# A fused transformer layer on one core: banks for the norm transposes, tables for additions and norms, order of the late norms

## The chip, the cores and the metric

The kernel runs on one core of a Trainium2 chip. The metric is the device time of one execution in microseconds (us), the median of several executions. The engines are TensorE (PE, and PEld for its weight loads), VectorE (DVE), ScalarE (ACT), GpSimd (POOL) and SyncE (SP, which issues most transfers). Each runs its own instructions in order; between engines the order is made by semaphores only.

## What is computed

The input x is 16 x 64 x 512 in float32, that is 1024 tokens of 512 features, handled as 8 tiles of 128 tokens.

```
x = x + cross_attention(layernorm(x), ctx, mask)      # 16 heads, 1601 context rows per batch
x = x + self_attention(layernorm(x))                  # w_qkv + b_qkv, low-rank terms on q and v, w_proj + b_proj
x = x + moe(layernorm(x))                             # gate: gelu(x @ wg1 + bg1) @ wg2 + bg2, softmax, top 2 of 20
```

The self attention works on each batch of 64 tokens alone, so a tile of 128 tokens holds two batches. The mixture of experts multiplies each token with the 512 x 512 matrices of its two best experts.

## The kernel before

Every float32 product is made of three products of rounded halves (`mm3`, lines 178 to 181), so each operand is kept as a high half (ScalarE copies it, L728) and a low half (VectorE subtracts, L1051). A product of one tile with a 512 x 512 weight is 12 matmuls (L179 to L181) into one PSUM bank of 512 columns. PSUM has 8 banks, `pb[0]` to `pb[7]`.

**Cross attention** fills the first 480 us and is not touched. **Before the steps** (lines 1344 to 1374 on VectorE) the layernorm of the second attention is made: residual addition and statistics per tile, factors on GpSimd (`factors`, L1617 and L1618), the norm on ScalarE (L878), a transpose on TensorE (L185), the halves, and the products that make queries and keys. `weight2(2, 1)` is VectorE's low half of the key weight, 128x2048; it stands ahead of `norm_lo(4)` and `norm_lo(5)`, and `keys2` waits for it.

**The second attention** is a loop over 14 steps, with three stages of eight tiles laid over one another:

- step s: scores of tile s (`a_scores`, L540, banks 4 to 7), the softmax on VectorE (L1380, L1386), ScalarE's exponential (L965), sums on VectorE and scaling on GpSimd (L1640);
- step s for tile s-1: the weights are turned (`a_turn`, L550) into banks 2 and 3, and ScalarE copies each bank (semaphore `a_t2`);
- step s for tile s-2: the product with the values (`a_values`, L566, in columns of banks 4 to 7), whose result ScalarE copies (L983) and VectorE halves (L1423, semaphore `v_h2`).

**Beside** them stand dense uses of TensorE, in a table `beside` (lines 679 to 685), three lists a step: values `v2`, output products `pj` (L582), norm transposes `n2` (L586) and the gate products `g1` (lines 591 to 597). They take banks 0 and 1 in turn, in the order of the table (line 691). A use waits until the use before it in the same bank has been read: `before` looks that up. Who reads what is in `done`: a `pj` is read by VectorE's residual addition (L1405, semaphore `v_x2`), a `v2` by ScalarE's copy, an `n2` by VectorE's low half (`v_n2`), a `g1` by `gelu`.

The addition for `pj` i stands one step later than the product, behind that step's softmax on VectorE, and ahead of the `n2` halves of the step; after it come the statistics, the factors on GpSimd, the norm on ScalarE one step later than the product (`norms(step - 1)`), behind the copies L983, and its transpose `n2` at the end of that step.

The order of the last steps before: `pj` 5, 6 and 7 stand in steps 9, 10 and 11, `n2` 4 and 5 in steps 9 and 10, the first gate product in step 11, `n2` 6 and 7 in step 12, the second gate product in step 13. On ScalarE `gelu(0)` comes in step 11 ahead of the norm of tile 7, the high half of expert weight 1 (`we_hi(1)`) at the end of step 12, then `gelu(1)`. On VectorE the low half `we_lo(1)` (L1436) stands behind the loop and ahead of the wait for the logits (L1448). `gelu` is a line of its own (L937) with a table load. SyncE loads the expert weights in a queue; those of 1 to 8 start when `p_a2` reaches 8, the last `a_values`.

**After the steps** come the logits (L617), a chain of small VectorE instructions (L1448 to L1505), GpSimd's 16 scatters of tokens (L1656), 20 or more expert blocks, and the gathers and last additions.

Of the kernel before, what the change touches and what calls it, by code (L numbers as in the profile page):

```python
# [17 lines left out]
def perceiver(nc, t, out):  # L18
# [9 lines left out]
    with root:  # L28
# [223 lines left out]
        def tensor(pe):  # L252
# [291 lines left out]
            def a_turn(i):  # L544
                for h in range(2):
                    pe.wait_ge(S["g_p2"], 2 * i + h + 1)
                    if i:
                        pe.wait_ge(S["a_t2"], 2 * i - 1 + h)
                    for j in range(4):
                        last = pe.transpose(pb[2 + h][:, j * 128:(j + 1) * 128],  # L550
                                            p2[i % 2][:, 4 * h + j].rearrange("p b k -> p (b k)"), ident)
                    last.then_inc(S["p_t2"], 1)
# [18 lines left out]
            def dense(what, i):  # L571
                if what == "qd":
                    queries2(1, i - 4)
                elif what == "kT":
                    keys2(1, i - 4)
                elif what == "v2":
                    values2(i)
                elif what == "pj":
                    pe.wait_ge(S["v_w2"], 2)
                    pe.wait_ge(S["v_h2"], i + 1)  # L580
                    pe.wait_ge(*before("pj", i))
                    project(i, wh[0], pb[bank_of("pj", i)]).then_inc(S["p_pj"], 1)  # L582
                elif what == "n2":
                    pe.wait_ge(S["a_nx"], 8 + i + 1)
                    pe.wait_ge(*before("n2", i))
                    turn4(pe, pb[bank_of("n2", i)], lambda k: xrow[:, i, k * 128:(k + 1) * 128]).then_inc(S["p_n2"], 1)  # L586
                else:
                    pe.wait_ge(S["v_g1"], 1)
                    pe.wait_ge(S["v_n2"], 8 + 4 * i + 3)
                    pe.wait_ge(*before("g1", i))  # L590
                    for c in (slice(0, 384), slice(384, 512)):
                        if c.start:
                            pe.wait_ge(S["v_n2"], 8 + 4 * i + 4)
                        for k in range(4):
                            last = mm3(pe, pb[bank_of("g1", i)][:, c], [w[:, k, :] for w in g1],
                                       [v[:, k, i * 512 + c.start:i * 512 + c.stop] for v in xu], k == 0, k == 3)
                    last.then_inc(S["p_g1"], 1)
# [76 lines left out]
            while guards:  # L674
# [11 lines left out]
        step_of = {use: step for step, parts in enumerate(beside) for part in parts for use in part}  # L686
        STEPS = len(beside)
        ring = [("o", i) for i in range(EARLY, 8)] + [("qd", m) for m in range(4)]
        ring += [use for m in range(4) for use in (("wl", 4 + m), ("kT", m))] + [("qd", 4)]
        place = [(("wl", k), 4 + k) for k in range(4)] + [(use, n % 3) for n, use in enumerate(ring)]  # L690
        place += [(use, n % 2) for n, use in enumerate([use for step in beside for part in step for use in part])]
        bank = dict(place)
        done = {"wl": ("v_wl", 0), "o": ("v_x1", 0), "kT": ("a_kT", 0), "v2": ("a_v2", 0),
                "pj": ("v_x2", 0), "n2": ("v_n2", 8), "g1": ("a_gelu", 0)}
# [31 lines left out]
        def scalar(act):  # L726
# [214 lines left out]
            def beside_read(uses):  # L941
                for what, i in uses:
                    if what == "qd":
                        queries2(1, i - 4)
                    elif what == "kT":
                        keys2(1, i - 4)
                    elif what == "v2":
                        values2(i)
                    elif what == "n2":
                        act.wait_ge(S["p_n2"], i + 1)  # L950
                        copy(xu[0][:, :, i * 128:(i + 1) * 128], kview(pb[bank_of("n2", i)])).then_inc(S["a_n2"], 1)
                    elif what == "g1":
                        gelu(i)

            def norms(step):
                for i in range(8):
                    if step_of["pj", i] == step:
                        norm(8 + i, i, xrow[:, i, 0:D])

            for step in range(STEPS):  # L960
                if step < 8:
                    i = step
                    pv = p2[i % 2].rearrange("p t b k -> p (t b k)")
                    act.wait_ge(S["v_sm"], 2 * i + 2)
                    act.activation(pv, pv, ACT.Exp, scale=SCALE).then_inc(S["a_e2"], 1)  # L965
                beside_read(beside[step][0])
                if 0 <= step - 1 < 8:
                    i = step - 1
                    for h in range(2):
                        act.wait_ge(S["p_t2"], 2 * i + h + 1)  # L970
                        if i >= 2:
                            act.wait_ge(S["p_a2"], i - 1)
                        else:
                            act.wait_ge(S["p_wl"], 8)
                        copy(pt2[:, i % 2, 4 * h:4 * h + 4, :].rearrange("p a c -> p (a c)"),
                             pb[2 + h][:, :]).then_inc(S["a_t2"], 1)
                beside_read(beside[step][1])
                if 0 <= step - 2 < 8:
                    i = step - 2
                    c = slice(i * 128, i * 128 + 128)  # L980
                    act.wait_ge(S["p_a2"], i + 1)
                    for g in range(4):
                        ins = act.activation(xu[0][:, g, c].rearrange("p (b q) -> p b q", b=2), turned2[:, :, g // 2, g % 2],  # L983
                                             ACT.Identity, bias=bl[:, 4 + g:5 + g])
                        if g % 2:
                            ins.then_inc(S["a_h2"], 1)
                norms(step - 1)
                beside_read(beside[step][2])
                if step == 3:
                    act.wait_ge(S["d_g1"], 32)  # L990
                    copy(g1[0][:, :, :], g1raw).then_inc(S["a_g1"], 1)
                if step == 5:
                    we_hi(0)
                if step == 12:
                    we_hi(1)

            act.wait_ge(S["v_lg"], 1)
            act.activation(pr[:, :, :], pr[:, :, :], ACT.Exp).then_inc(S["a_le"], 1)
# [48 lines left out]
        def vector(dve):  # L1047
# [286 lines left out]
            def weight2(j, n):  # L1334
                dve.wait_ge(S["a_w2"], n)
                rest(wh[j][1][:, :, :], raw[:, 0], wh[j][0][:, :, :]).then_inc(S["v_w2"], 1)
# [24 lines left out]
            norm_lo(2)  # L1361
            norm_lo(3)
            out_add(7)
            weight2(2, 1)
            norm_lo(4)
            norm_lo(5)
            queries2(0, 1)
            norm_lo(6)
            norm_lo(7)
# [27 lines left out]
            for step in range(STEPS):  # L1397
# [1 line left out]
                    i = step  # L1399
                    a_softmax(i)  # L1400
                for i in range(8):
                    if step_of["pj", i] == step - 1:
                        dve.wait_ge(S["g_xb"], i + 1)
                        dve.wait_ge(S["p_pj"], i + 1)
                        dve.tensor_tensor(x_sb[:, i, :], x_sb[:, i, :], pb[bank_of("pj", i)][:, :],  # L1405
                                          ALU.add).then_inc(S["v_x2"], 1)
                        dve.wait_ge(S["v_x2"], i + 1)
                        stat(i)
# [151 lines left out]
        def gpsimd(pool):  # L1560
# [70 lines left out]
                pool.wait_ge(S["g_xb"], i + 1)  # L1631
            for i in range(STEPS):
                for j in range(8):
                    if step_of["pj", j] == i - 1:
                        factors(8 + j, j)
                if i < 8:
                    pool.wait_ge(S["v_rl2"], i + 1)
                    for h in range(2):
                        pv = p2[i % 2][:, 4 * h:4 * h + 4].rearrange("p t b k -> p (t b) k")
                        pool.tensor_tensor(pv, pv, ls2[:, i % 3, 8 * h:8 * h + 8].unsqueeze(2).to_broadcast([128, 8, 64]),  # L1640
                                           ALU.mult).then_inc(S["g_p2"], 1)
                if i in (6, 7):
                    pool.wait_ge(S["a_we"], 1)
                    pool.wait_ge(d_we[0], 16)
                    for k in (2 * (i - 6), 2 * (i - 6) + 1):
                        ins = pool.tensor_tensor(wsplit[0][1][:, k, :], wraws[0][:, k, :],
                                                 wsplit[0][0][:, k, :].bitcast(f32), ALU.subtract)
                    if i == 7:
                        ins.then_inc(S["g_we"], 1)
# [312 lines left out]
```

## Time and profile before

| what | us |
|---|---|
| median of 3 runs | 831.63 (831.05 to 832.65) |
| the profiled execution's own time | 832.59 |
| its span, first to last instruction | 830.8 |
| PE busy | 723.9 (87%) |
| DVE busy | 402.4 (48%) |
| ACT busy | 365.1 (44%) |
| POOL busy | 279.7 (34%) |

All durations come from the one profiled execution. "Busy" is the time in which an engine works; the chain that ended last has PE in 75% of the span. A line of the timeline gives start, duration, engine, line of the kernel, operation, out<-in with shapes, count, and in brackets the idle time before it with what ended it. Matmuls overlap in the profile, so a start to the next start is the pace.

### The profile page before, as it was taken

Reading aid. Unit: us, or ns where it says so; the run is one execution under the profiler, and the core shown is the slowest. Engines: PE = TensorE matmul, PEld = TensorE weight load, DVE = VectorE, ACT = ScalarE, POOL = GpSimd, SP = SyncE. Lnnn points to the kernel's source line nnn. Section 1 sums busy time; section 2 is a strip of 40 time slices with the busy share of each in tenths; the row PEclk is TensorE's granted clock in tenths of the full one; section 3 lists DMA queues with packets and bytes.
Section 4 is the critical chain, followed back from the end, with each engine's and each line's share of the span. In section 5 each row is a group of like instructions: output and inputs, shape, how many; then the busy total and the mean of one; then the engine's idle time right before and its main releaser. Section 6 shows DMA issues by size and latency. Waiting matters only on the chain.

```text
span 830.8 us, 16898 instructions
## 1 busy us (share of the span) xinstructions
PE 723.9 (87%) x6819; PEld 586.9 (71%) x6819; DVE 402.4 (48%) x846; ACT 365.1 (44%) x665; POOL 279.7 (34%) x249
## 2 busy tenths in 40 slices
PE   0899999999999999999999999999686653989880
PEld 0797888878888888888788777877564621766660
DVE  4823443354444345444543283446533452677755
ACT  1425534545434454445453163444442400688750
POOL 0005223444224442245542236022321044243334
PEclk9999999999999999999999999999998755899995
DMA  9303321453322333101100021100007426499938
GB/s 292 120 1 44 86 54 38 131 136 85 86 82 56 85 85 85 41 2 40 42 2 2 4 66 64 52 2 2 2 1 285 191 101 203 153 374 415 390 126 305
DMA packets 43783, 89.98 MB, mean 108 GB/s; under 512 B 7370, under 2 KB 26314, under 8 KB 39214
## 3 DMA queue, kind: packets, MB, share of 16 engines
q1 hardware_dynamic: 40254, 77.46, 29.5%
q0 software_dynamic: 3440, 11.31, 3.4%
q8 instruction: 58, 0.95, 0.5%
q14 instruction: 31, 0.25, 0.1%
HBM read 66.18 MB, written 22.65 MB: 107 GB/s over the span
## 4 chain that ended last, share of the span: by engine, by line
PE 75%; DMA 8%; DVE 6%; issue 6%; ACT 3%; POOL 2%; SPq 0%; POOLq 0%; DVEq 0%; ACTq 0%
PE bank L179 20%; PE bank L181 18%; PE bank L180 18%; PE bank L185 9%; PE bank L338 4%; PE bank L315 3%; DMA xi<-scratch_xg 3%; POOL scratch_xg L1656 2%; DMA scratch_ys<-xm,xi 2%; DVE x_sb L1555 1%; DMA scratch_ys<-hT,xi 1%; DMA scratch_xg<-acc,si 1%; PE bank L550 1%; DMA wr<-scratch_ys 1%; ACT xu L728 1%
## 5 line engine op out<-in xcount | busy, mean ns | idle before, releaser
L1583 POOL TENSOR_SCALAR pp<-pp,rl 128x400 f32<-128x400 f32 x128 | 163.8, 1298 | 234.8 <-DVE rl L1148 234.8
L179 PE MATMUL bank<-chi,wk 128*128 128x400 f32 x256 | 93.5, 365 | 0.0
L1204 DVE COPY pt<-bank 128x512 f32<-128x512 f32 x64 | 44.3, 692 | 99.4 <-PE bank L185 99.3
L811 ACT ACTIVATE pp<-pp,acc 128x400 f32<-128x400 f32 x128 | 79.0, 619 | 28.0 <-DVE acc L1237 27.7
L1237 DVE CUSTOM_DVE_ANT_0 pp<-bank,cap 128x400 f32<-128x400 f32 x128 | 66.8, 569 | 46.5 <-PE bank L315 46.5
L181 PE MATMUL bank<-chi,wk 128*128 128x400 f32 x256 | 88.3, 345 | 0.0
L180 PE MATMUL bank<-clo,wk 128*128 128x400 f32 x256 | 88.3, 345 | 0.0
L179 PE MATMUL bank<-wv,chi 128*128 128x512 f32 x200 | 83.5, 417 | 0.0
L179 PE MATMUL bank<-wh,xu 128*128 128x512 f32 x152 | 66.9, 440 | 16.8 <-DVE x_sb L1405 15.8
L181 PE MATMUL bank<-wv,clo 128*128 128x512 f32 x200 | 78.5, 393 | 0.0
L180 PE MATMUL bank<-wv,chi 128*128 128x512 f32 x200 | 78.5, 393 | 0.0
L728 ACT ACTIVATE pt<-bank 128x512 f32<-128x512 f32 x64 | 38.2, 597 | 76.4 <-PE bank L185 75.3
L185 PE MATMUL bank<-cst,pp 128*128 128x128 f32 x512 | 67.2, 274 | 0.6 <-DVE x_sb L1181 0.6
L181 PE MATMUL bank<-wh,xu 128*128 128x512 f32 x152 | 63.6, 418 | 0.0
L180 PE MATMUL bank<-wh,xu 128*128 128x512 f32 x152 | 63.5, 418 | 0.0
L185 PEld LDWEIGHTS bank<-cst,pp 128*128 128x128 f32 x512 | 58.5, 140 | 5.8 <-issue 0.8
L728 ACT ACTIVATE vv<-bank 128x512 f32<-128x512 f32 x50 | 29.1, 583 | 64.9 <-PE bank L181 64.9
L179 PEld LDWEIGHTS bank<-wv,chi 128*128 128x128 f32 x200 | 37.5, 188 | 27.9 <-issue 19.4
L1051 DVE TENSOR_TENSOR xu<-bank,xu 128x512 fp32r<-128x512 f32 x44 | 29.9, 687 | 44.7 <-ACT xu L728 44.7
L1135 DVE COPY kk<-bank 128x400 f32<-128x400 f32 x32 | 18.4, 575 | 63.3 <-PE bank L181 63.3
L179 PEld LDWEIGHTS bank<-wh,xu 128*128 128x128 f32 x152 | 30.8, 203 | 24.7 <-issue 18.4
L180 PEld LDWEIGHTS bank<-clo,wk 128*128 128x128 f32 x256 | 48.3, 189 | 0.0
(224 smaller groups left out, 1424.4 us busy)
## 6 DMA issues: line engine op xcount, KB each, us to landing
wr<-in_We SPq DMA_DIRECT2D x19, 1024.0 KB, 8.9
craw<-in_ctx SPq DMA_DIRECT2D x16, 800.0 KB, 5.7
scratch_xg<-zero SPq DMA_DIRECT2D x20, 448.0 KB, 8.3
raw<-in_We SPq DMA_DIRECT2D x8, 1024.0 KB, 7.6
xi<-scratch_xg SPq DMA_DIRECT2D x28, 258.0 KB, 6.6
wr<-scratch_ys SPq DMA_DIRECT2D x8, 512.0 KB, 7.3
x_sb<-in_x SPq DMA_DIRECT2D x2, 1024.0 KB, 12.1
out_dram<-x_sb SPq DMA_DIRECT2D x8, 256.0 KB, 4.2
```

The costliest lines, as they stand in the source:

```text
L179: pe.matmul(o, lhs[0], rhs[0], start=start, stop=False)
L180: pe.matmul(o, lhs[0], rhs[1], start=False, stop=False)
L181: return pe.matmul(o, lhs[1], rhs[0], start=False, stop=stop)
L185: last = pe.transpose(bank[0:n, k * 128:(k + 1) * 128], of(k), ident)
L315: last = pe.matmul(scores[64 * c:64 * c + 64, j, :], qc[r, 2 * half + c, 64 * b:64 * b + 64], kk[r, 2 * half + c, :], start=True, stop=True)
L338: last = pe.matmul(turned[32 * j:32 * j + 32, g, :], vv[:, (25 * (n // 8) + 3 * (n % 8) + i4) % 4, 128 * g + 32 * j:128 * g + 32 * j + 32] ...
L728: return act.activation(dst, src, ACT.Copy)
L811: act.activation(frame(p8), frame(p8), ACT.Exp, bias=bias, scale=-1.0, accum_out=total).then_inc(S["a_exp"], 1)
L1051: return dve.tensor_tensor(dst, src, hi.bitcast(f32), ALU.subtract)
L1204: dve.tensor_copy(pt[:, p8 % 4, :, :].rearrange("p a c -> p (a c)"), at("t", 8 * (n - 1) + p8)[:, :]).then_inc(S["v_pt"], 1)
L1237: dve.tensor_tensor_reduce(out=frame(p8), in0=scores[:, p8 % 4, :], in1=cap[:, :], scale=-1.0, scalar=nm[:, b, p8:p8 + 1] if seg else 3e38 ...
L1583: pool.tensor_scalar(frame(p8), frame(p8), rl[:, n % 2, p8:p8 + 1], None, ALU.mult).then_inc(S["g_pn"], 1)
```

## The change

On TensorE the transposes `n2` no longer take banks 0 and 1 but banks 2 and 3, those of the turned weights. Each waits for ScalarE's last copy of a turned half in its bank and for the `n2` two before it; each `a_turn` in turn waits for the last `n2` of its bank. Banks 0 and 1 go round among the other uses. Tables say in which step an addition and a norm stand; the addition for `pj` 7 moves from step 12 to step 11. `n2` 6 moves into step 11, `n2` 7 is alone in step 12. On ScalarE the norms of the steps from 8 on come ahead of the copies L983, `gelu(0)` moves to the end of step 12, and `we_hi(1)` comes behind `gelu(1)`. On VectorE `weight2(2, 1)` comes behind `norm_lo(4)` and `norm_lo(5)`. GpSimd's factors follow the table of additions. `we_lo(1)` keeps its place on VectorE.

```diff
--- before.py
+++ after.py
@@ tensor: a_turn
                     if i:
                         pe.wait_ge(S["a_t2"], 2 * i - 1 + h)
+                    turned = [j for j in range(8) if j % 2 == h and step_of["n2", j] <= i]
+                    if turned:
+                        pe.wait_ge(S["v_n2"], 8 + turned[-1] + 1)
@@ tensor: dense
                 elif what == "n2":
                     pe.wait_ge(S["a_nx"], 8 + i + 1)
-                    pe.wait_ge(*before("n2", i))
+                    pe.wait_ge(S["a_t2"], 2 * min(step_of["n2", i] - 1, 7) + i % 2 + 1)
+                    if i >= 2:
+                        pe.wait_ge(S["v_n2"], 8 + i - 1)
@@ tables
-                  ([("pj", 6)], [], [("n2", 5)]), ([("pj", 7)], [], [("g1", 0)]),
-                  ([], [], [("n2", 6), ("n2", 7)]), ([], [], [("g1", 1)])]
+                  ([("pj", 6)], [], [("n2", 5)]), ([("pj", 7)], [], [("g1", 0), ("n2", 6)]),
+                  ([], [], [("n2", 7)]), ([], [], [("g1", 1)])]
+        add_at = {i: step_of["pj", i] + (i < 7) for i in range(8)}
+        norm_at = {i: step_of["pj", i] + 1 for i in range(8)}
...
-        place += [(use, n % 2) for n, use in enumerate([use for step in beside for part in step for use in part])]
+        dense_uses = [use for step in beside for part in step for use in part if use[0] != "n2"]
+        place += [(use, n % 2) for n, use in enumerate(dense_uses)]
+        place += [(("n2", i), 2 + i % 2) for i in range(8)]
@@ scalar
-                    elif what == "g1":
-                        gelu(i)
...
-                    if step_of["pj", i] == step:
+                    if norm_at[i] == step:
...
                 beside_read(beside[step][1])
+                if step >= 8:
+                    norms(step)
                 if 0 <= step - 2 < 8:
...
-                norms(step - 1)
+                if step < 8:
+                    norms(step)
                 beside_read(beside[step][2])
...
                 if step == 12:
-                    we_hi(1)
+                    gelu(0)
+            gelu(1)
+            we_hi(1)
@@ vector, ahead of the steps
             out_add(7)
-            weight2(2, 1)
             norm_lo(4)
             norm_lo(5)
+            weight2(2, 1)
             queries2(0, 1)
@@ vector, in the steps
-                    if step_of["pj", i] == step - 1:
+                    if add_at[i] == step:
@@ gpsimd
-                    if step_of["pj", j] == i - 1:
+                    if add_at[j] == i:
```

## Rows read from the trace of the kernel before

**Rows 1.** Stretches: each engine's busy us, PE clock share, DMA share, GB/s.

```profile
583.60:597.80 14.20, 10.49 (x169) 8.44 (x168) 7.30 (x15) 6.87 (x11) 5.26 (x6) 0.88 0.01 2
630.00:637.40 7.40, 5.26 (x18) 4.04 (x19) 2.38 (x6) 1.41 (x2) 0.74 (x2) 0.77 1.00 404
660.90:673.70 12.80, 2.23 (x8) 1.67 (x8) 10.56 (x60) 2.14 (x2) 0.00 (x0) 0.50 0.01 2
```

**Rows 2.** Waits of PE, 574 to 664 us: total, times, longest.

```profile
PE bank L179 <- DVE x_sb L1405: 15.8, 6, 3.7
PE bank L185 <- ACT acc L878: 4.3, 2, 2.3
```

**Rows 3.** Timeline, steps 6 to 8: start, us, instruction, [idle before].

```profile
587.51 1.06 ACT L965 ACTIVATE acc<-acc 128x1024 f32<-128x1024 f32 x1 [1.41 <-DVE acc L1386]
...
588.22 0.47 PE L179 MATMUL bank<-wh,xu 128*128 128x512 f32 x1 [3.71 <-DVE x_sb L1405]
...
592.63 0.60 PE L550 MATMUL bank<-cst,p2b 128*128 128x128 f32 x4
...
614.12 0.47 PE L179 MATMUL bank<-wh,xu 128*128 128x512 f32 x1 [2.10 <-DVE x_sb L1405]
...
617.00 1.03 PE L550 MATMUL bank<-cst,p2b 128*128 128x128 f32 x8
```

**Rows 4.** Timeline, one norm's way in step 10.

```profile
637.23 0.60 PE L185 MATMUL bank<-cst,acc 128*128 128x128 f32 x4
637.86 0.60 ACT L728 ACTIVATE xu<-bank 128x512 fp32r<-128x512 f32 x1 [2.27 <-PE bank L185]
638.49 0.69 DVE L1051 TENSOR_TENSOR xu<-bank,xu 128x512 fp32r<-128x512 f32 x1 [4.65 <-ACT xu L728]
639.10 0.68 DVE L1405 TENSOR_TENSOR x_sb<-x_sb,bank 128x512 f32<-128x512 f32 x1
...
641.05 0.55 POOL L1617 TENSOR_TENSOR rstd<-rstd,cst 128x1 f32<-128x1 f32 x1 [6.31 <-DVE nbias L1311]
...
641.90 0.81 ACT L878 ACTIVATE acc<-x_sb,nbias,rstd 128x512 f32<-128x512 f32 x1 [3.45 <-POOL nbias L1618]
```

**Rows 5.** Timeline around the two gate products, steps 11 to 13.

```profile
644.34 0.34 PE L179 MATMUL bank<-xu,g 128*128 128x384 f32 x1
...
647.75 0.62 PE L185 MATMUL bank<-cst,acc 128*128 128x128 f32 x4
647.98 1.28 ACT L937 ACT_TABLE_LOAD   x1 [5.26 <-PE bank L181]
...
650.71 1.12 PE L185 MATMUL bank<-cst,acc 128*128 128x128 f32 x4 [2.34 <-ACT acc L878]
...
652.02 0.66 PE L179 MATMUL bank<-xu,g 128*128 128x384 f32 x1 [0.19 <-DVE xu L1051]
```

**Rows 6.** Timeline ahead of the steps, last norms of the first attention.

```profile
494.99 0.55 POOL L1617 TENSOR_TENSOR rstd<-rstd,cst 128x1 f32<-128x1 f32 x1 [3.79 <-DVE nbias L1311]
...
498.69 2.28 DVE L1051 TENSOR_TENSOR wh<-raw,wh 128x2048 fp32r<-128x2048 f32 x1
...
498.86 2.53 POOL L1617 TENSOR_TENSOR rstd<-rstd,cst 128x1 f32<-128x1 f32 x1 [3.04 <-DVE nbias L1311]
...
504.43 0.63 PE L185 MATMUL bank<-cst,acc 128*128 128x128 f32 x4 [1.24 <-DVE xu L1051]
```

**Rows 7.** Timeline, from the gate to the first scatter.

```profile
652.36 1.90 ACT L728 ACTIVATE wh<-raw 128x2048 fp32r<-128x2048 f32 x1
...
654.30 2.29 DVE L1436 TENSOR_TENSOR wh<-raw,wh 128x2048 fp32r<-128x2048 f32 x1 [1.11 <-ACT wh L728]
...
658.12 0.69 ACT L937 ACTIVATE xm<-bank,gw 128x512 f32<-128x512 f32 x1 [3.86 <-issue]
...
660.91 0.33 DVE L1448 TENSOR_TENSOR pr<-bank,bro 128x160 f32<-128x160 f32 x1 [4.32 <-PE bank L617]
...
674.04 1.27 POOL L1656 DMA_INDIRECT scratch_xg<-acc,si  x1 [26.64 <-DVE si L1505]
```

## The prediction

> **What bounds the kernel now.** I began with the page of the profile: PE is busy in 87% of the span and holds 75% of the chain that ended last, so a wait of PE on this chain is time to be won. The page's slices then show where PE isn't full: in the second attention's late steps, and behind them in the routing. The windows by stage put numbers on it: from 583.6 to 597.8 us PE works 10.49 of 14.2 us at a granted clock of 0.88, from 630.0 to 637.4 it works 5.26 of 7.4 us at 0.77 [rows 1]. The list of waits names the causes: six matmuls waited 15.8 us in all for VectorE's residual addition L1405, and norm transposes waited 4.3 us for ScalarE's norm L878, twice [rows 2]. The timeline shows what such a wait is. In step 6 the product `v2` 5 sits in the bank that held `pj` 1, whose addition stands behind the softmax of step 6; it idles 3.71 us. It then runs until 592.63, 4.41 us for 12 matmuls, where the same product in step 8 takes from 614.12 to 617.00, 2.88 us, behind a wait of 2.10 [rows 3]. So the longer wait costs a second time, in the clock: within the slow product the granted clock is at its lower level, 1.2 GHz in place of 2.4. Routing can't start before the second gate product, so all of this is on the path to the end.
>
> **The change, part by part.** All times are of the profiled execution.
>
> *The additions no longer gate the next use.* With the norm transposes out of banks 0 and 1, `v2` and `pj` alternate: `v2` i has bank 0, `pj` bank 1. A `v2` now waits for ScalarE's copy of the `v2` before it, and a `pj` in steps 6 to 8 for an addition that VectorE makes while PE is at `v2`, the turn and the values. The later ones follow in the same manner: `pj` 5 waits for the copy of `v2` 7, `pj` 6 for the addition of `pj` 4, `pj` 7 for that of `pj` 5, each some 3 us earlier than needed. All six waits go: 15.8 us [rows 2]. The slow clock was met on four products (`v2` 5 and 6, `pj` 6 and 7), each 4.41 - 2.88 = 1.53 us too long [rows 3]. I credit three, 4.6 us, and leave one (`pj` 7) slow, for a reason below.
>
> *The end of the steps.* Before, `gelu(0)` with its table load of 1.28 us stands ahead of the norm of tile 7, so the last transpose waits 2.34 us; it takes 1.12 us, its like 0.62; and the second gate product runs from 652.02 until ScalarE's gelu at 658.12, 6.1 us, where the first took from 644.34 to 647.75, 3.41 us [rows 5, 7]. With the norm first, what goes is the 4.3 us of both norm waits [rows 2], 0.5 us, 2.7 us of the slow gate product, and the 0.19 us ahead of it: 7.7 us. New ones come instead.
>
> *The new waits.* PE now meets the norms' own chain. Its price is read in step 10: from the transpose at 637.23 over the copy, the low half, the addition, the statistics and the factors to the norm, which ends at 641.90 + 0.81 = 642.71: 5.5 us [rows 4]. Before, the waits for additions hid most of it. After: from `n2` 3 to `n2` 4 PE has the transposes (0.5), `pj` 5 (2.9) and the values (0.8), 4.2 us, so it waits 1.3. From `n2` 4 to `n2` 5 it has 0.5 + 2.9 = 3.4 us, and ScalarE has the copies of tile 7's values ahead of `n2` 4's, about 0.3, so it waits 2.4. From `n2` 5 to `n2` 6 stand `pj` 7 and the first gate product, over 6 us: nothing. From `n2` 6 to `n2` 7 ScalarE copies (0.6) and then norms (0.8), against 0.5 on PE: 1.4 with the starts between (0.63 from a transpose to its copy) [rows 4]. In steps 6 and 7 the exponential (until 588.57 [rows 3]) stands ahead of ScalarE's copies, and the norm comes out about level with PE's product: I put 0.2 each. In sum 5.5 us. The bounds: nothing at all, if ScalarE is quicker than I order it, and 2.1 us for each of five, the size of the old short waits, 10.5.
>
> *The turned banks.* `a_turn` now waits for the low half of the last transpose. In step 6 that is `n2` 0's, whose copy and half are the first things ScalarE and VectorE do behind it, some 2 us ahead of the turn: nothing, covered by `v2`. If that cover went, the price would be the 1.3 us from a transpose's start to its half (637.86 + 0.63 + 0.69 from 637.23 is 1.95, less the 0.6 of the transpose) [rows 4].
>
> *Norms ahead of the value copies, from step 8 on.* The copies L983 start some 0.8 us later; their reader `pj` stands a step behind. Nothing, and about 0.5 us of the norm waits would be longer without it, which the sum has already.
>
> *VectorE ahead of the steps.* The factors of tile 7 take GpSimd 2.53 us, against 0.55 for those of tile 6, and they run beside VectorE's 2.28 us of `weight2` [rows 6]: it holds them up. Norm and transpose of tiles 6 and 7 come late, and PE idles 1.24 us [rows 6]. With `weight2` behind the two halves, tile 7's factors take 0.55 and that wait goes: 1.24 us. PE is full from there to the steps, so it carries through. `weight2` ends about 505.3; `keys2`, its reader, starts some 5 us later, and the load of the projection weight that SyncE holds for it has more than 5 us as well. Nothing for both; without this cover up to 2 us.
>
> *`we_hi(1)` behind `gelu(1)`.* This is a new cost. VectorE's `we_lo(1)` stands ahead of its wait for the logits and needs `we_hi(1)`. Before, both were done by 656.59, under the gate product. Now from the end of `gelu(1)` they take 1.90 + 2.29 = 4.2 us, while the logits took 660.91 - 658.81 = 2.1 [rows 7]. The logits' chain on VectorE comes 2.1 us late, and with it the first scatter, now at 674.04 [rows 7]. The table load of 1.28 us for the exponential follows `we_hi(1)` and is hidden by `we_lo(1)`.
>
> **The sum.** Gone: 15.8 + 4.6 + 7.7 + 1.24 = 29.3. New: 5.5 + 2.1 = 7.6. Net 21.7 us. Behind L1448 the order is unchanged and moves as a whole. The span goes from 830.8 to 809.1, the profiled execution from 832.6 to 810.9; the median of the runs is 1.0 under that execution, so 831.6 - 21.7 = **809.9 us**.
>
> **The clock, and the rivals.** Before, single waits of 2.10 us left the clock at its upper level (twice), while one of 2.0 (4.3 less 2.3, [rows 2]) just ahead of one of 2.1, or 3.7 alone, brought it down. The new 1.3 and 2.4 stand 3.7 us apart, so I leave `pj` 7 slow. If it isn't, 808.4; if the second gate product is slow too, 809.9 + 3.2 = 813.1. All this is the forecast's case.
>
> *The clock falls at every new wait.* The five waits stand where five groups of matmuls start: `v2` 6, `v2` 7, `pj` 6, `pj` 7 and the second gate product. Four more than I count: 3 x 1.53 + 3.2 = 7.8, so 817.7. For it: clock and waits went together in four of the six cases. Against it: two waits of 2.10 us did nothing, and three of the new ones are shorter [rows 3]. The Trainium skill (TensorE: Matmul & The Clock Gate, section on psum-queue depth-cycling) says that frequent short idling between groups of matmuls makes the clock swing; by that rule, this is the case that would come.
>
> *The weights' transfers set the end.* The loads of expert weights start at the last `a_values` and fill the DMA engines (share 1.00, 404 GB/s) [rows 1]. If the end hung on them, only what is gained up to there counts: 2 x 3.71 + 2 x 2.10 + 3.1 - 0.4 + 1.2 = 15.5, so 816.1. Against it: from 660.9 to 673.7 the DMA share is 0.01 [rows 1], the loads were done well ahead of the scatters.
>
> *Slower.* The waits only change their name: the turn waits for the halves in banks 2 and 3 and PE idles as long as before. Then `we_lo(1)` decides: it is the one added cost on the path behind the steps, 2.1 us [rows 7]. It gives 831.6 + 2.1 = 833.7, slower as soon as the steps and the part ahead of them win under 2.1 us together. That also is the case in which the change doesn't do what it says. Against it: VectorE and ScalarE idle while PE waits, and the banks' new readers are early.
>
> **How the numbers follow.** Forecast's case 0.78, clock at every wait 0.10, transfers 0.04, slower 0.03, and 0.05 for less new waiting than 5.5 us, towards 804. The range takes in the forecast's 808.4 to 813.1, half of the new waits' bound below, and about 3 us for new waits at their upper bound: 806 to 816, which leaves out less than 0.2. A measurement of this kernel can tell 0.2%, 1.7 us, from no change. Faster 0.96, same 0.01, slower 0.03.
>
> **What would show it.** Right: no wait of PE on L1405, or nearly none; waits of L185 for L878 of some 1.3, 2.4 and 1.4 us; `gelu(1)` about 24 us earlier but L1448 only 22, with L1436 directly ahead of it; the factors of tile 7 at 0.55 us. Wrong: PE waits at L550 for L1051, granted clock under 0.9 throughout the late steps, or a later stage that is longer than before.

## The result and the profile after

The changed kernel takes 806.09 us (median of 4 runs, 804.15 to 806.81), the kernel before in the same runs 831.35 (831.05 to 832.65): ratio 0.969, 95% interval 0.967 to 0.971. Five more rounds gave 805.77 us and a ratio of 0.9717 (0.9690 to 0.9745). The forecast was 809.9, from 806 to 816. The time stands on the low edge of that range, and the ratio just outside it: 0.969 of the median that I started from, 831.63, is 805.9. The direction was right; the gain was 25.3 us where I had 21.7. Where the other 3.6 us come from is taken apart below.

The windows of the changed kernel (columns as in [rows 1]; lines below L549 have moved by up to 12, so L1405, L1436, L1448 and L878 are now L1417, L1448, L1460 and L887):

```profile
574.00:600.00 26.00, 26.00 (x431) 21.24 (x430) 20.51 (x44) 16.37 (x31) 11.27 (x15) 1.00 0.01 3
600.00:620.00 20.00, 16.19 (x199) 12.85 (x198) 10.00 (x28) 7.65 (x17) 4.32 (x8) 0.98 0.42 158
620.00:640.00 20.00, 12.78 (x80) 11.64 (x79) 9.44 (x27) 10.37 (x11) 1.49 (x4) 0.84 0.77 308
```

From 574 to 600 us PE has no gap, at the full clock. Before, in the steps 6 and 7, the stretch from 583.6 to 597.8 us ran at 0.88 with a quarter of the time idle [rows 1]. The list of waits of PE, 560 to 640 us (total, times, longest), stands against [rows 2]:

```profile
PE bank L185 <- ACT acc L887: 5.2, 3, 2.4
PE bank L622 <- ACT xm L946: 0.8, 1, 0.8
PE bank L540 <- DVE xu L1435: 0.2, 1, 0.2
```

No wait for a residual addition is left. The norm waits are three, 5.2 us in all. The timeline of PE has them one by one, with what follows each, against [rows 3, 5]:

```profile
598.74 0.60 PE L185 MATMUL bank<-cst,acc 128*128 128x128 f32 x4
...
599.10 0.48 PE L179 MATMUL bank<-wh,xu 128*128 128x512 f32 x1
...
612.16 0.66 PE L185 MATMUL bank<-cst,acc 128*128 128x128 f32 x4 [1.42 <-ACT acc L887]
...
612.57 0.48 PE L179 MATMUL bank<-wh,xu 128*128 128x512 f32 x1
...
617.96 0.66 PE L185 MATMUL bank<-cst,acc 128*128 128x128 f32 x4 [2.39 <-ACT acc L887]
...
618.38 0.48 PE L179 MATMUL bank<-wh,xu 128*128 128x512 f32 x1
...
622.80 0.34 PE L179 MATMUL bank<-xu,g 128*128 128x384 f32 x1
...
628.18 0.66 PE L185 MATMUL bank<-cst,acc 128*128 128x128 f32 x4 [1.39 <-ACT acc L887]
...
628.59 0.42 PE L179 MATMUL bank<-xu,g 128*128 128x384 f32 x1
```

The turned banks never make PE wait: no line of `a_turn` stands in the list. The waits ahead of `n2` 4, 5 and 7 are 1.42, 2.39 and 1.39 us; I had worked out 1.3, 2.4 and 1.4. Ahead of `n2` 1 and 2 there is none (I had 0.2 each). `pj` 7 runs from 618.38 to 622.80, 4.42 us, the slow product that I had left in the sum. The second gate product starts at 628.59 and its gelu at 632.29, 3.7 us, against 6.1 before.

The end, against [rows 7]:

```profile
632.29 0.69 ACT L946 ACTIVATE xm<-bank,gw 128x512 f32<-128x512 f32 x1 [0.82 <-issue]
632.88 1.90 ACT L737 ACTIVATE wh<-raw 128x2048 fp32r<-128x2048 f32 x1
...
634.81 2.29 DVE L1448 TENSOR_TENSOR wh<-raw,wh 128x2048 fp32r<-128x2048 f32 x1 [4.61 <-ACT wh L737]
637.02 0.32 DVE L1460 TENSOR_TENSOR pr<-bank,bro 128x160 f32<-128x160 f32 x1
...
650.14 1.27 POOL L1668 DMA_INDIRECT scratch_xg<-acc,si  x1 [24.28 <-DVE si L1517]
```

The expert pair now stands on the way: ScalarE's half, then VectorE's, and L1460 starts directly behind, 4.73 us after `gelu(1)`, where it was 2.79. From L1460 to the first scatter it is 13.12 us, before 13.13.

Ahead of the steps, against [rows 6], the power of tile 7 (the first instruction of GpSimd's `factors`) takes 0.55 us, and `weight2` comes after the two halves:

```profile
498.32 0.55 POOL L1629 TENSOR_TENSOR rstd<-rstd,cst 128x1 f32<-128x1 f32 x1 [3.00 <-DVE nbias L1323]
...
502.29 2.98 DVE L1063 TENSOR_TENSOR wh<-raw,wh 128x2048 fp32r<-128x2048 f32 x1
```

In its new place `weight2` itself takes 2.98 us for 2.28: GpSimd's additions of 128x512 (L1642) run beside it from 499.09 us on. It ends at 505.27, still ahead of its reader.

**Where the time went.** Certain lines can be found in every trace, so each execution can be cut into stretches. A: from the power of tile 7 (GpSimd) to the sixth softmax's first line (VectorE's `mx`, step 5). B: from there to `gelu(1)`. C: from there to the logits' first line on VectorE. D: from there to the first load of scattered tokens. E: from there to the first gather. All are differences of starts in the timelines, in us, one profiled execution each; what remains to the span lies behind E:

| kernel | start of A | A | B | C | B + C | D | E | span |
|---|---|---|---|---|---|---|---|---|
| before | 498.86 | 76.79 | 82.47 | 2.79 | 85.26 | 40.69 | 109.28 | 830.8 |
| changed | 498.32 | 75.18 | 58.79 | 4.73 | 63.52 | 40.53 | 107.66 | 805.0 |
| changed, again | 497.72 | 75.22 | 58.75 | 4.73 | 63.48 | 40.63 | 109.09 | 805.6 |
| front_only | 497.05 | 75.17 | 82.37 | 2.89 | 85.26 | 40.66 | 107.94 | 825.7 |
| front_undone | 497.40 | 76.87 | 58.74 | 4.73 | 63.47 | 40.55 | 108.43 | 806.6 |
| banks_only | 497.74 | 76.79 | 61.53 | 3.05 | 64.58 | 40.67 | 109.11 | 808.3 |
| end_undone | 497.77 | 75.18 | 62.00 | 2.80 | 64.80 | 40.70 | 109.90 | 807.7 |
| norms_behind | 497.94 | 75.17 | 59.09 | 4.72 | 63.81 | 40.69 | 108.25 | 805.2 |
| pair_early | 497.72 | 75.17 | 60.76 | 2.74 | 63.50 | 40.83 | 107.29 | 803.9 |
| hi_early | 498.44 | 75.18 | 58.77 | 2.74 | 61.51 | 40.74 | 107.61 | 803.3 |
| filler | 497.81 | 75.18 | 57.21 | 4.73 | 61.94 | 40.56 | 108.04 | 803.3 |
| hi_fill3 | 497.92 | 75.17 | 57.23 | 3.32 | 60.55 | 40.95 | 107.92 | 801.9 |
| hi_fill1 | 497.93 | 75.20 | 57.19 | 3.21 | 60.40 | 40.72 | 108.08 | 801.7 |

A, B and C repeat to 0.1 us where nothing of theirs was touched. The start of A moves by 1.8 us and E by 2.6 us between executions, with no regard to the edit. So the change is worth 1.61 us in A and 21.74 in B and C, 23.35 in all. The other 2.45 us between these two spans lie elsewhere: 1.62 in E, 0.54 ahead of A, 0.16 in D and 0.13 behind E. banks_only, end_undone, norms_behind and filler were executed once only (810.12, 809.49, 806.99 and 805.06 us); of them the stretches count, not the time.

### The profile page after: what moved, and what is told of

It is laid out like the page before. It is cut to its first block, busy times and chain, and to the rows that moved or that the text cites. A ratio compares the mean times of both kernels' runs of the same rounds, so it can differ in the third digit from the quotient of the medians.

```text
span 805.0 us, 16898 instructions
## 1 busy us (share of the span) xinstructions
PE 714.5 (89%) x6819; PEld 580.1 (72%) x6819; DVE 402.4 (50%) x846; ACT 364.4 (45%) x665; POOL 279.7 (35%) x249
## 4 chain that ended last, share of the span: by engine, by line
PE 76%; DMA 8%; DVE 6%; issue 5%; POOL 2%; ACT 2%; SPq 0%; POOLq 0%; DVEq 0%; ACTq 0%
PE bank L179 20%; PE bank L181 18%; PE bank L180 18%; PE bank L185 9%; PE bank L338 4%; PE bank L315 3%; DMA xi<-scratch_xg 3%; POOL scratch_xg L1668 2%; DMA scratch_ys<-xm,xi 2%; DVE x_sb L1567 1%; DMA scratch_ys<-hT,xi 1%; PE bank L553 1%; DMA scratch_xg<-acc,si 1%; PE bank L540 1%; DMA wr<-scratch_ys 1%
## 5 line engine op out<-in xcount | busy, mean ns | idle before, releaser
L179 PE MATMUL bank<-wh,xu 128*128 128x512 f32 x152 | 65.2, 429 | 0.7 <-DVE xu L1063 0.7
L181 PE MATMUL bank<-wh,xu 128*128 128x512 f32 x152 | 61.8, 407 | 0.0
L180 PE MATMUL bank<-wh,xu 128*128 128x512 f32 x152 | 61.3, 403 | 0.0
L179 PEld LDWEIGHTS bank<-chi,wk 128*128 128x128 f32 x256 | 48.2, 188 | 0.0
```

What stands on the lines that cost most here:

```text
L179: pe.matmul(o, lhs[0], rhs[0], start=start, stop=False)
L180: pe.matmul(o, lhs[0], rhs[1], start=False, stop=False)
L181: return pe.matmul(o, lhs[1], rhs[0], start=False, stop=stop)
```

## The experiments

**again**: the changed kernel unchanged.

> The changed kernel once more, in more rounds. If the 1.9 us that the span lost behind L1448 and the 0.5 us ahead of 496 us are chance of one execution, this run has them at another size: the stretch from L1448 to the end anywhere from 168 to 170 us, and the ratio to the kernel before nearer 0.971 (a gain of 24 us). If they belong to the change, the stretch is again 168.0 us and the ratio 0.969.

805.77 us against 829.53 (17 runs of the kernel before), ratio 0.9717 (0.9690 to 0.9745). The last stretches are another size, E 109.09 in place of 107.66, while A to C are the same within 0.05. The ratio is the 0.971 that was expected if the surplus of the first measurement is chance, and E, at 109.09, is as long as in the kernel before (109.28). The intervals of the two ratios overlap, so the times alone wouldn't show it. The kernel before itself ran from 825.36 to 831.65 in these 17 runs, so an edit of 1 or 2 us has to be read in the stretches, not in the times.

**front_only**: in the kernel before,

```diff
             out_add(7)
-            weight2(2, 1)
             norm_lo(4)
             norm_lo(5)
+            weight2(2, 1)
```

> Only the low half of the key weight behind norm_lo(4) and norm_lo(5), in the kernel before. My account: the power of tile 7 takes 0.55 us in place of 2.53, PE's wait of 1.24 us goes, and the gain is 1.2 us, up to 1.6 if a wait costs PE more than the idle time that the profile shows. Rival, nothing is gained, since VectorE's queue is as long as before and PE waits for a later half: 0 us. Rival, the power is slow for another reason and stays at 2.5 us.

829.24 us, ratio 1.0003 (0.9983 to 1.0023). The time doesn't show the gain: 1.6 us would be a ratio of 0.998. Only the stretches do. The timeline of GpSimd has the power at 0.55 us:

```profile
497.05 0.55 POOL L1617 TENSOR_TENSOR rstd<-rstd,cst 128x1 f32<-128x1 f32 x1 [2.78 <-DVE nbias L1311]
```

and A is 75.17 against 76.79, 1.62 us. The wait is gone and the steps, B and C, are those of the kernel before. The transposes around that wait, before and then here:

```profile
499.42 1.03 PE L185 MATMUL bank<-cst,acc 128*128 128x128 f32 x8
...
504.43 1.23 PE L185 MATMUL bank<-cst,acc 128*128 128x128 f32 x8 [1.24 <-DVE xu L1051]
```

```profile
497.61 1.03 PE L185 MATMUL bank<-cst,acc 128*128 128x128 f32 x8
...
501.23 1.04 PE L185 MATMUL bank<-cst,acc 128*128 128x128 f32 x8
```

From start to start it is 5.01 us and 3.62: the wait cost 1.39, not the 1.24 of its idle time, and the eight transposes behind it took 0.19 more. That is the 1.6 us.

**front_undone**: the same edit backwards, in the changed kernel.

> The changed kernel with that low half back ahead of norm_lo(4). It should lose what front_only wins, 1.2 to 1.6 us against the changed kernel (about 807.5). If the gain ahead of the steps is swallowed by the steps, it loses nothing.

807.73 us, ratio 0.9743 (0.9713 to 0.9773), about 2 us above the changed kernel in the same sitting; A is 76.87. The two engines beside one another:

```profile
497.31 2.29 DVE L1063 TENSOR_TENSOR wh<-raw,wh 128x2048 fp32r<-128x2048 f32 x1
497.40 2.61 POOL L1629 TENSOR_TENSOR rstd<-rstd,cst 128x1 f32<-128x1 f32 x1 [2.78 <-DVE nbias L1323]
```

VectorE's `weight2` starts at 497.31. GpSimd's power of one column starts at 497.40, takes 2.61 us and ends 0.4 us behind it. Two edits in opposite directions give 1.6 and 1.7 us in A: the front is settled at 1.6.

**banks_only**: the kernel before with the hunks of `a_turn`, of `n2` on TensorE and of `place`; nothing else.

> In the kernel before only the banks: the norm transposes in 2 and 3 with their waits, all tables, ScalarE's order and the front as before. My account: the six waits for L1405 go (15.8 us, and some 0.2 each for the restart), three or four slow products become full (4.6 or 6.1), a norm wait of some 2.4 us comes ahead of n2 5; the end (gelu(0) ahead of the norm of tile 7, slow gate product) stays. From the sixth softmax to L1448 about 66.5 us in place of 85.3. Rival, the banks without the order of the norms and gelu give only half: 75 us.

B and C together 64.58, 20.7 us less than before. The banks alone bring the gain, more than I gave them. Waits of PE and then its timeline:

```profile
PE bank L185 <- ACT acc L885: 4.9, 3, 2.3
```

```profile
613.72 0.66 PE L185 MATMUL bank<-cst,acc 128*128 128x128 f32 x4 [1.93 <-ACT acc L885]
...
619.32 0.66 PE L185 MATMUL bank<-cst,acc 128*128 128x128 f32 x4 [0.60 <-ACT acc L885]
...
628.94 1.11 PE L185 MATMUL bank<-cst,acc 128*128 128x128 f32 x4 [2.34 <-ACT acc L885]
...
630.20 0.66 PE L179 MATMUL bank<-xu,g 128*128 128x384 f32 x1
```

The norm wait ahead of `n2` 4 is 1.93 us, the one ahead of `n2` 5 only 0.60: here the clock fell in `pj` 6 (5.19 us from its start to that of `n2` 5), not in `pj` 7. Since the norm's chain runs meanwhile, the slow product hides in what PE would have waited. That is most of the 1.9 us by which the stretch beats my figure, so some 1.6 of the 20.7 us hang on where the clock fell in this one execution. The end is the old one: 2.34 us ahead of `n2` 7 and a slow gate product.

**end_undone**: the changed kernel with the old end.

```diff
-                  ([("pj", 6)], [], [("n2", 5)]), ([("pj", 7)], [], [("g1", 0), ("n2", 6)]),
-                  ([], [], [("n2", 7)]), ([], [], [("g1", 1)])]
+                  ([("pj", 6)], [], [("n2", 5)]), ([("pj", 7)], [], [("g1", 0)]),
+                  ([], [], [("n2", 6), ("n2", 7)]), ([], [], [("g1", 1)])]
-        add_at = {i: step_of["pj", i] + (i < 7) for i in range(8)}
+        add_at = {i: step_of["pj", i] + 1 for i in range(8)}
...
+                    elif what == "g1":
+                        gelu(i)
...
-                    gelu(0)
-            gelu(1)
-            we_hi(1)
+                    we_hi(1)
```

> The changed kernel with the end of the steps as before: n2 6 and 7 both in step 12, the addition of pj 7 in step 12, gelu(0) in step 11 ahead of the norm of tile 7, we_hi(1) ahead of gelu(1). My account: PE's last norm wait is 2.3 us again in place of 1.4, the second gate product is slow if the clock falls in that wait (3 us), and the 2.0 us of the expert pair come back. From the sixth softmax to L1460 64.2 us with a slow gate product, about 61.5 without, against 63.5 in the changed kernel. Rival, the new end is what brings most of the gain: over 68 us.

```profile
628.42 0.66 PE L185 MATMUL bank<-cst,acc 128*128 128x128 f32 x4 [2.35 <-ACT acc L887]
...
629.68 0.41 PE L179 MATMUL bank<-xu,g 128*128 128x384 f32 x1 [0.60 <-issue]
```

The last norm wait is 2.35 us, the gate product is slow from its sixth matmul on (0.50 to 0.52 us each where it is 0.34), and C is back at 2.80. B + C is 64.80, 0.6 over what I had expected: the new end is worth 1.3 us net, 3.2 in B, less 1.9 in C. It isn't what brings the gain.

**norms_behind**: the changed kernel with one call of `norms(step)` behind the copies L992 in all steps.

> The changed kernel with the norms behind the value copies in all steps. My account: the wait ahead of n2 4 grows from 1.4 to 1.9 us, as in banks_only, the others stay: stretch 64.0 us. Rival, the order sets more than that since n2 3's norm is late too: 65 us or more. Rival, nothing: 63.5.

```profile
612.23 0.66 PE L185 MATMUL bank<-cst,acc 128*128 128x128 f32 x4 [1.93 <-ACT acc L887]
...
617.83 0.66 PE L185 MATMUL bank<-cst,acc 128*128 128x128 f32 x4 [2.19 <-ACT acc L887]
```

1.93 us ahead of `n2` 4, as expected, but the next wait shrinks from 2.39 to 2.19: the stretch is 63.81. The norms' precedence is worth 0.3 us. This run is also the counterpart of banks_only. Both take 6.07 us from `n2` 3 to `n2` 4, with the same wait of 1.93 us, and 5.60 us from `n2` 4 to `n2` 5. But here `pj` 6 is at full clock and `pj` 7 slow, there `pj` 6 was slow and `pj` 7 full. So the length of a wait alone doesn't say whether the clock falls behind it; what decided between these two was not found.

**pair_early**: both halves of expert weight 1 in step 11.

```diff
                 if step >= 8:
                     norms(step)
+                if step == 11:
+                    we_hi(1)
...
             gelu(1)
-            we_hi(1)
...
+                if step == 11:
+                    we_lo(1)
                 norm2_lo(beside[step][2])
...
-            we_lo(1)
```

> The changed kernel with both halves of expert weight 1 in step 11 (ScalarE's behind the norm of tile 6, VectorE's behind the statistics of tile 7), off the way from the gate to the logits. My account: that way costs 2.1 us in the changed kernel, L1460 comes 2.0 us earlier, the time falls by 2.0 to 804.1. Rival, the first scatter doesn't depend on it, or something else is as late (the exponential's table load, transfers): 0 us. Rival, the pair delays the norm of tile 7 or the halves of n2 6, so that PE's last wait grows from 1.4 to over 3 us: 0 us or slower.

806.55 us, ratio 0.9730 (0.9702 to 0.9758), B + C 63.50: nothing. C fell to 2.74 as my account has it, and B rose by 2.0. The timeline of VectorE, GpSimd and PE:

```profile
624.70 2.29 DVE L1405 TENSOR_TENSOR wh<-raw,wh 128x2048 fp32r<-128x2048 f32 x1 [0.41 <-ACT wh L737]
...
625.00 2.05 POOL L1632 TENSOR_TENSOR nbias<-nbias,rstd 128x1 f32<-128x1 f32 x1
...
627.95 1.03 PE L185 MATMUL bank<-cst,acc 128*128 128x128 f32 x4 [1.78 <-ACT acc L887]
...
628.63 0.67 PE L179 MATMUL bank<-xu,g 128*128 128x384 f32 x1
...
629.10 0.52 PE L180 MATMUL bank<-xu,g 128*128 128x384 f32 x1
```

VectorE's subtraction from 624.70 holds up GpSimd's factor of tile 7, 2.05 us where it takes 0.19. The norm is late, the wait ahead of `n2` 7 is 1.78 in place of 1.39, and in this somewhat longer wait the clock falls: the gate's matmuls take 0.52 us. So the rival was right on the time, though not on the sizes: it is 0.4 us of wait, not over 1.6, and the other 1.6 us are the clock. The Trainium skill (SBUF — State Buffer, section "SBUF: two separate sides") says that VectorE with two inputs in SBUF and GpSimd share a port pair that one of them holds for a whole instruction; 2.05 against 0.19 here and 2.61 against 0.55 above agree.

**hi_early**: ScalarE's half alone in step 11, the first and the second hunk above.

> The changed kernel with ScalarE's half of expert weight 1 alone moved into step 11, behind the norm of tile 6; VectorE's half stays behind the loop and finds it done. My account: gelu(1) stays where it is against the end of the steps (PE's last norm wait 1.4 us, no slow gate product), and from gelu(1) to L1460 it is 2.8 us in place of 4.7, so from the sixth softmax (the mx of step 5) to L1460 61.5 us in place of 63.5. Rival, pair_early gave its 2.0 us back since ScalarE's copy is in the way: then gelu(1) comes 2 us late again and the stretch stays at 63.5.

B + C 61.51, the 61.5 that I had; 805.08 us, ratio 0.9689 (0.9663 to 0.9716). The times of the changed kernel, 806.09 and 805.77, come from other sittings and lie too near to show 2 us; the stretch does.

```profile
623.48 1.90 ACT L737 ACTIVATE wh<-raw 128x2048 fp32r<-128x2048 f32 x1
...
630.21 2.28 DVE L1449 TENSOR_TENSOR wh<-raw,wh 128x2048 fp32r<-128x2048 f32 x1
...
632.39 0.69 ACT L946 ACTIVATE xm<-bank,gw 128x512 f32<-128x512 f32 x1 [0.82 <-issue]
...
635.13 0.33 DVE L1461 TENSOR_TENSOR pr<-bank,bro 128x160 f32<-128x160 f32 x1 [2.64 <-PE bank L622]
```

VectorE's half follows the last half of a norm, where GpSimd has nothing to do, and is done 2.6 us ahead of the logits. The cost of the pair on the path is shown: 2.0 us.

**filler**: on TensorE,

```diff
                 elif what == "n2":
+                    if i == 5:
+                        pe.wait_ge(*before("pj", 7))
+                        for k in range(8):
+                            pe.matmul(pb[bank_of("pj", 7)][:, :], xu[0][:, k % 4, 768:896], wh[0][0][:, k % 4, :],
+                                      start=True, stop=True)
                     pe.wait_ge(S["a_nx"], 8 + i + 1)
```

> The changed kernel with eight matmuls of no use ahead of n2 5, in the bank that pj 7 will overwrite: PE's wait of 2.4 us for the norm is filled with work, the norm comes no sooner. My account (the clock is a cost of its own): pj 7 takes 2.9 us in place of 4.4, the stretch from the sixth softmax to L1460 62.0 us in place of 63.5. Rival, pj 7 is slow because of ScalarE, VectorE or the transfers beside it, not because PE was idle: still 4.4 us, 63.5 or more.

The same stretch of `pj` 7 in the windows, the changed kernel first:

```profile
618.40:622.80 4.40, 4.40 (x15) 3.46 (x13) 2.38 (x6) 0.70 (x2) 0.74 (x2) 0.61 1.02 425
```

```profile
617.80:620.70 2.90, 2.90 (x16) 2.39 (x15) 1.93 (x3) 0.60 (x1) 0.00 (x0) 1.00 1.02 424
```

and the filled kernel's timeline ahead of it:

```profile
617.41 0.66 PE L185 MATMUL bank<-cst,acc 128*128 128x128 f32 x4 [0.58 <-ACT acc L892]
...
617.83 0.48 PE L179 MATMUL bank<-wh,xu 128*128 128x512 f32 x1
```

The norm comes no sooner, the wait left is 0.58 us, and `pj` 7 takes 2.84 us at full clock in place of 4.42 at 0.61. The transfers beside it are as busy as before (share 1.02) and do nothing to it. B + C is 61.94 against the 62.0 expected. So the fall costs 1.6 us of its own, and without the idle time it doesn't come. In hi_fill1 and hi_fill3 below, `pj` 7 behind such matmuls is at full clock too.

**hi_fill3** and **hi_fill1**: hi_early with such matmuls ahead of `n2` 4, 5 and 7, or ahead of `n2` 5 only.

> hi_early with such matmuls in all three norm waits (5 ahead of n2 4, 8 ahead of n2 5, 5 ahead of n2 7). The costs add: 2.0 + 1.5 = 3.5 us under the changed kernel, stretch 60.0 us, time about 802.3. Rival, the fillers run over the norms' arrival or bring VectorE's and ScalarE's reads behind them: stretch 61 us or more.

> hi_early with the eight matmuls ahead of n2 5 only. The 2.0 us and the 1.5 us add, and PE has its other waits as in filler, so that the logits' matmuls stay at 2.0 us: stretch 60.0 us in place of hi_fill3's 60.6, time 802.3. Rival, the clock falls in the logits here as well, or the two don't add: 60.5 us or more.

802.87 us, ratio 0.9663 (0.9639 to 0.9687), and 802.94, ratio 0.9664 (0.9639 to 0.9688). Both beat the changed kernel by some 3 us; B + C is 60.55 and 60.40, where 60.0 was expected of each. The 2.0 and the 1.6 us add but for 0.4 to 0.6, which is in C, 3.3 and 3.2 in place of 2.74. In hi_fill1 the logits are

```profile
631.06 2.43 PE L627 MATMUL bank<-gw,xm 128*128 128x20 f32 x16 [0.83 <-ACT xm L951]
```

2.43 us where the changed kernel has 1.96 (in hi_fill3 2.54): the clock now falls there, to 0.75 in the mean of 630.9 to 633.8 us. The rival of hi_fill1 was right in this. In filler and in hi_early, each with one of the two edits, the logits stay at 1.96; why they don't here wasn't found. Three fillings are no better than one: of the three waits of the changed kernel only the one of 2.39 us had a slow product behind it.

## Why the prediction was right or wrong

**What failed, in short.** The mechanism held. Three terms of the sum were too small or too large by 1.6 us together: the six waits (15.8 us, measured 16.9), the front (1.24, measured 1.6) and the expert pair (2.1, measured 1.9). The step "behind L1448 the order is unchanged and moves as a whole" took the rest of the kernel as a constant, and that put the measurement past the edge of the range.

**Right, by its own steps.** The six waits for L1405 went. Of four slow products one is left, and it is `pj` 7. The chain of 5.5 us from one transpose to the next norm gave the three larger new waits within 0.12 us each; the two of 0.2 didn't come, so it is 5.2 in all for 5.5. The turned banks never made PE wait. The pair behind `gelu(1)` cost 1.9 us for 2.1, and hi_early shows the same 2.0 from the other side. GpSimd's power was held up by `weight2` and no longer is.

**Too small: the term "15.8 us".** I took the idle time that the list of waits gives as the price of a wait. Starts give more. Before, the transpose ahead of the wait of 2.10 us started here,

```profile
611.43 0.60 PE L185 MATMUL bank<-cst,acc 128*128 128x128 f32 x4
```

and `v2` 7 at 614.12, 2.69 us later [rows 3]; in the changed kernel they are 0.36 us apart (598.74 and 599.10). The wait cost 2.33 us, 0.23 more than its idle time: it is counted from the modelled end of the matmuls before, which overlap those behind when nothing waits. Four such waits are 0.9 us; the two of 3.71 cost 3.79 each, together 0.2 more. With this 1.1 and the 0.16 us by which the pair cost less than 2.1, the 20.46 us for the steps (21.7 less the front) become 21.7; 21.74 was measured. What is left of B, three products back at full clock (4.6) and the old end less the new waits (7.7 - 5.5 = 2.2), comes to 6.8 us from start to start, as forecast. Within it errors cancel: the two new waits of 0.2 us didn't come, the others cost a little more than their idle time, and the second gate product won 2.4 us for 2.7.

**Too small: the front's 1.24 us.** The same kind of error: 1.39 us from start to start and 0.19 in the transposes behind the wait, 1.6 us in two experiments.

**The step that failed for the range: "behind L1448 the order is unchanged and moves as a whole".** The order does move as a whole: D is equal within 0.4 us. But the time isn't a constant: E ranges over 2.6 us in thirteen executions, and the stretch ahead of A over 1.8. I had set my range from the costs of the edit alone and from one execution of the kernel before. Repeatable gain 23.35, so 808.3 from 831.6: inside the range and 1.6 from the forecast. The rest of the way to 806.1 is of the size of this scatter. Between sittings the changed kernel hardly moved (806.09 and 805.77), while the kernel before stood at 831.35, then 829.53, 830.67 and 831.23. The intervals of 0.969 and 0.972 overlap, so the difference between the two ratios can be chance; no run isolates it. What in the cross attention and the expert blocks makes the scatter was not looked into.

**The rivals.** *Clock at every wait*: it fell at one of three. The Trainium skill's rule (TensorE: Matmul & The Clock Gate, on psum-queue depth-cycling) foresees such swinging; here waits of 1.42 and 1.39 us left the clock up. No length of a wait divides the cases: behind 1.78 us the clock fell in pair_early, behind 1.93 it fell in banks_only and not in norms_behind, and behind the four waits of 2.10 in the kernel before it fell twice. *Transfers set the end*: no, the gain of A, B and C, 23.35 us, reached the first scatter whole. *Slower*: the pair was on the path as priced, but B won over ten times as much, 23.7 us for 1.9.

## What to carry to other kernels

When two kinds of use share a ring of buffers, the slow reader of one sets the pace of both; giving the short uses a place away from them was most of the gain here, 20.7 of 23.35 us. Price a wait from start to start, not by its idle time, and ask what the clock does behind it: filling a wait of 2.4 us with matmuls of no use won 1.6 us. And before a range is written, run the kernel before often enough to know what its untouched stretches do.

## What the runs showed of the hardware

- A fall of the clock costs nothing where the next thing PE waits for is late anyway: in banks_only `pj` 6 was slow and the next norm wait was 0.60 us, in norms_behind it was at full clock and the wait 2.19; from `n2` 4 to `n2` 5 it is 5.60 us in both.
- A fall that was avoided at one place can be followed by one at another: with `pj` 7 at full clock and the pair moved, the logits took 2.43 and 2.54 us for 1.96. With only one of the two edits they stayed at 1.96, so this isn't the filling's doing alone.
- VectorE's subtraction of 128x2048, with both inputs in SBUF, holds up a one-column instruction of GpSimd until its own end, 2.05 us for 0.19 and 2.61 for 0.55, so it belongs where GpSimd is not on the path. The other way round it is less: beside GpSimd's additions of 128x512 it took 2.98 us for 2.28.
